# A recurrent column scan: n's bias in the tanh, z's matmuls ahead of n's, and the reset product of one half between the mix and the state of the other

## The chip, the cores and the metric

The kernel runs on one core of a Trainium2 chip. The metric is the time of one execution on the device in microseconds (us). Five engines work on their own instruction queues, each in order: TensorE (PE; its weight loads are shown apart, as PEld), VectorE (DVE), ScalarE (ACT), GpSimd (POOL) and SyncE (SP), which here only starts transfers. An instruction that waits for a semaphore holds everything behind it on its engine. Lines such as L1344 are lines of the kernel before, unless the text says that they are of the kernel after.

## The reference

The input `x` has 16 images of 32 channels and 64 x 64 pixels, in fp32. Four layers follow one another, each of the form `x = x + layer(group_norm(x))`: a 3x3 convolution, a recurrent scan over the columns of the image, and two multiplications in the Fourier domain. The change touches the scan alone:

```python
def _cell(prev_col, cur_col, weight_ih, bias_ih, weight_hh, bias_hh):
    pad = jnp.pad(prev_col, ((0, 0), (1, 1), (0, 0)))
    x = jnp.concatenate([pad[:, :-2], pad[:, 1:-1], pad[:, 2:]], axis=-1)
    i_vals = jnp.einsum('bhk,ok->bho', x, weight_ih) + bias_ih
    h_vals = jnp.einsum('bhc,oc->bho', cur_col, weight_hh) + bias_hh
    r_i, z_i, n_i = jnp.split(i_vals, 3, axis=-1)
    r_h, z_h, n_h = jnp.split(h_vals, 3, axis=-1)
    r = jax.nn.sigmoid(r_i + r_h)
    z = jax.nn.sigmoid(z_i + z_h)
    n = jnp.tanh(n_i + r * n_h)
    return n * z + cur_col * (1.0 - z)
```

Column 0 is the first state. Columns 1 to 63 each take the state of the column before (with the neighbouring pixels above and below) and their own values.

## The kernel before

**Layout.** The 128 partitions hold four interleaved row groups of 32 channels. A column of 16 images is 128 x 256 elements; it is cut into two halves of 8 images, h = 0 and 1, 128 x 128 elements each. The halves don't depend on each other. So the scan is 63 columns x 2 halves = 126 half-steps, and each engine does the halves in turn.

**One half-step** of half h and column w, by engine:

- PE (`half_step`, L700): `from_column` (L697) multiplies the current column for r, z and n into PSUM and reports `h_sum`. It waits until r's and z's gates and the reset product of the column before have been read. Then, when the state's edges (`sedge_ready`, from ACT) and its straddled copy (`lower_ready`, from POOL) are there, `from_state` (L690) multiplies the state of the column before, in three passes of four 32-column matmuls: for r, n and z, in this order; each reports its sum. In the trace a matmul in fp32 shows as two, so a pass over three gates has 24 records.
- ACT (`scan_step`, L1031), in this order in its queue: r's gate of half 0 (L1021), z's gate of half 0 (L1025), the edges of the state of half 1 of the column before (L1016), the tanh of half 0 (L1029, into PSUM), then the same with the halves exchanged.
- DVE (`new_state`, L1341), five instructions for a half: the reset product gr x PSUM (L1344), the addition with n's bias and n's sum (L1347), the keep product (z - 1) x column (L1352), the mix n x z (L1355), and the state, mix minus keep (L1360), which also waits for POOL and ACT to have read the state before it.
- POOL (`scan_step`, L527): the straddled copy of the new state, mix minus keep once more for 64 partitions (L531), as soon as mix and keep are there; then the addition of the state into the image (L525).
- SP starts two transfers per column, which bring the edge rows of a later column (L440), when both halves' `h_sum` are reported.

**What sets the order.** Nothing but the order in which the code is written for each engine, and the semaphores. DVE runs `new_state(0, w)` and then `new_state(1, w)`, three columns in a loop body, 21 times. Behind the scan DVE, ACT and POOL copy the image for the transform, when the last additions into the image (`added`) are done.

Of the kernel before, what the change touches and what calls it, by code (L numbers as in the profile page):

```python
# [15 lines left out]
ALU = mybir.AluOpType  # L16
ACT = mybir.ActivationFunctionType

B, C, H, W = 16, 32, 64, 64
# [61 lines left out]
def program(nc, x, conv_w, conv_b, scan_wi, scan_wh, scan_b, w2, w3, w9, out_b, group_d, const_d, out):  # L81
    ctx = ExitStack()
    with ctx:
        def sem(name):
            return ctx.enter_context(nc.semaphore(name))
# [16 lines left out]
        psum = ctx.enter_context(nc.psum_tensor("psum", [P, 8, 512], F32))  # L102
# [9 lines left out]
        def sm(n):  # L112
            at[0] += n
            return small[:, at[0] - n:at[0]]
# [18 lines left out]
        bias_s = sm(6)  # L133
# [5 lines left out]
        HB = B * H4 // 2  # L139
        off = 4 * H4 * PADW  # L140

        def scan_buf():
            nonlocal off
            off += HB
            return spec[:, off - HB:off]
# [11 lines left out]
        gr, gz, pre1, pre2, keep, mix = [[scan_buf() for _ in range(2)] for _ in range(6)]  # L157
        gn = [psum[:, 4 * h + 2, HB:2 * HB] for h in range(2)]
# [10 lines left out]
        def straddled(h, q, first):  # L169
            return straddle[h][q].rearrange("p (b h) -> p b h", h=H4 + 1)[:, :, first:first + H4]  # L170
# [51 lines left out]
        r_sum, z_sum, n_sum = [[sem(f"{g}_sum{h}") for h in range(2)] for g in "rzn"]  # L222
        r_gate, z_gate, n_gate = [[sem(f"{g}_gate{h}") for h in range(2)] for g in "rzn"]
        reset_done = [sem(f"reset_done{h}") for h in range(2)]
        pre_ready = [sem(f"pre_ready{h}") for h in range(2)]
# [392 lines left out]
        def _(pe):  # L618
# [53 lines left out]
            for g in range(4):  # L672
                for row in (C, 2 * C):
                    last = mm(psum[row:row + C, 5, P * g:P * g + P], bias_z[:, C * g:C * g + C], cm["ident"],
                              start=True, stop=True)
# [10 lines left out]
            def from_state(h, g, starts=False):  # L686

                moving = (straddled(h, slice(0, P), 0), state[h], state[h], straddled(h, slice(0, P), 1))
                for hm in (1, 2, 0, 3):
                    last = mm(psum[QUARTERS[hm], 4 * h + g, 0:HB], sv[:, g, QUARTERS[hm]], moving[hm],  # L690
                              start=starts, stop=True)
                return last

            def from_column(h, g, parity, stops=False):
                up, lo = edges_of(h, parity)
                for q, e in zip(QUARTERS, (up, up, lo, lo)):
                    last = mm(psum[q, 4 * h + g, 0:HB], sv[:, 3 + g, q], e, start=True, stop=stops)  # L697
                return last

            def half_step(h, w, parity, nth):  # L700
                if nth is None:
                    pe.wait_ge(cur_first[h], 32)
                else:
                    pe.wait_ge(cur_in[parity], nth * 32)
                    pe.wait_ge(r_gate[h], w - 1)
                    pe.wait_ge(z_gate[h], w - 1)
                    pe.wait_ge(reset_done[h], w - 1)
                from_column(h, 0, parity)
                from_column(h, 1, parity)
                from_column(h, 3, parity, True).then_inc(h_sum[h], 1)  # L710
                pe.wait_ge(sedge_ready[h], w)
                pe.wait_ge(lower_ready[h], w)
                from_state(h, 0).then_inc(r_sum[h], 1)
                from_state(h, 2, True).then_inc(n_sum[h], 1)
                from_state(h, 1).then_inc(z_sum[h], 1)

            pe.wait_ge(scan_w_in, 16 * 14)
            pe.wait_ge(bias_written, 2)
            pe.wait_ge(conv_added, 2 * B)
            half_step(0, 1, 1, None)  # L720
            pe.wait_ge(stat1, (NG - 1) * KGN + steps_all(GB - 1) + steps_all(1))
            half_step(1, 1, 1, None)
            with pe.Fori(0, (W - 4) // 4) as i:
                for k in range(4):
                    for h in range(2):
                        half_step(h, i * 4 + (k + 2), k % 2, i * 2 + (k // 2 + 1))
# [209 lines left out]
        def _(act):  # L936
            a = nc.scalar.activation
# [59 lines left out]
            for row, o in ((C, slice(P // 2, P)), (2 * C, slice(0, P // 2))):  # L997
# [11 lines left out]
                    bias=sh1[:, GB - 1:GB]).then_inc(columns_ready, 1)  # L1009
# [16 lines left out]

            def candidate(h, w):
                act.wait_ge(pre_ready[h], w)
                a(gn[h], pre2[h], ACT.Tanh).then_inc(n_gate[h], 1)  # L1029

            def scan_step(w):  # L1031
                reset_gate(0, w)
                update_gate(0, w)
                state_edges(1, w - 1)
                candidate(0, w)
                reset_gate(1, w)
                update_gate(1, w)
                state_edges(0, w)
                candidate(1, w)
# [140 lines left out]
        def _(dve):  # L1180
            v = nc.vector
# [156 lines left out]
                    dve.wait_ge(columns_ready, B)  # L1338
                v.tensor_copy(state[h], columns[:, h * HB:h * HB + HB]).then_inc(state_ready[h], 1)

            def new_state(h, w):  # L1341
                dve.wait_ge(r_gate[h], w)
                dve.wait_ge(h_sum[h], w)
                v.tensor_tensor(pre1[h], gr[h], psum[:, 4 * h + 3, 0:HB], ALU.mult).then_inc(reset_done[h], 1)  # L1344
                dve.wait_ge(reset_done[h], w)
                dve.wait_ge(n_sum[h], w)
                v.scalar_tensor_tensor(out=pre2[h], in0=psum[:, 4 * h + 2, 0:HB], scalar=bias_s[:, 2:3], in1=pre1[h],  # L1347
                                       op0=ALU.add, op1=ALU.add).then_inc(pre_ready[h], 1)
                dve.wait_ge(z_gate[h], w)
                dve.wait_ge(lower_ready[h], w)  # L1350

                v.scalar_tensor_tensor(out=keep[h], in0=gz[h], scalar=1.0, in1=columns[:, ds(w * (2 * HB) + h * HB, HB)],  # L1352
                                       op0=ALU.subtract, op1=ALU.mult).then_inc(keep_ready[h], 1)
                dve.wait_ge(n_gate[h], w)
                v.tensor_tensor(mix[h], gn[h], gz[h], ALU.mult).then_inc(mix_ready[h], 1)  # L1355
                dve.wait_ge(mix_ready[h], w)
                dve.wait_ge(keep_ready[h], w)
                dve.wait_ge(added[h], w)
                dve.wait_ge(sedge_ready[h], w)
                v.tensor_tensor(state[h], mix[h], keep[h], ALU.subtract).then_inc(state_ready[h], 1)  # L1360

            with dve.Fori(0, (W - 1) // 3) as i:
                for k in range(3):
                    for h in range(2):
                        new_state(h, i * 3 + (k + 1))


            dve.wait_ge(added[0], W)
# [90 lines left out]
            for half_ in range(2):  # L1459
                dve.wait_ge(l2_done, 2 * half_ + 2)  # L1460
                dve.wait_ge(sq_done, 2 * half_ + 3)
                if half_ == 0:

                    v.scalar_tensor_tensor(out=sq[0:C, :], in0=o[:, 0, 0, :], scalar=1.0, in1=shift[0:C, :],
                                           op0=ALU.mult, op1=ALU.add).then_inc(l2_added, 1)
# [6 lines left out]
                for sign, ri, dst in ((0.5, 0, col0[:, lo:hi, 0, :]), (0.5, 1, col0[:, lo:hi, 1, :]),  # L1472
# [3 lines left out]
                                           op0=ALU.mult, op1=ALU.add).then_inc(l2_added, 1)  # L1476
# [11 lines left out]
            def settle3():  # L1488
# [20 lines left out]
                                         op0=ALU.mult, op1=ALU.add))  # L1509
# [112 lines left out]
```

## Time and profile before

| | |
|---|---|
| median of 3 runs (lowest, highest) | 597.79 us (596.89, 597.91) |
| the profiled execution, its own time | 597.76 us |
| its span, first to last instruction | 595.9 us |
| mean granted TensorE clock | 0.988 of full speed |
| PE busy over the span | 539.8 us (91%) |
| DVE busy | 492.0 us (83%) |
| ACT busy | 396.7 us (67%) |
| POOL busy | 311.3 us (52%) |

The shares are means over stages with different limits, so they don't say what one stage is bound by. Inside the scan one looks at what each engine waits for: rows of a timeline give the start (us from the span's start), the duration, the engine, the line, the operation, what is written and read, and in brackets how long the engine had been idle and who released it. Where one engine's row starts a few hundredths behind another's end again and again, the two are links of a loop.

### The profile page before, as it was taken

How to read it: one execution, taken by the hardware profiler on the slowest of the kernel's cores; microseconds unless marked ns; L12 is line 12 of the kernel's file. 1: busy time of each engine (PE TensorE's matmuls, PEld its weight loads, DVE VectorE, ACT ScalarE, POOL GpSimd, SP SyncE). 2: the span in 40 equal slices, each digit the busy share in tenths (PEclk: the TensorE clock that was granted, in tenths of full speed). 3: DMA queues.
4: the chain of work that ended last, by engine and by line, in shares of the span. 5: the costliest groups of instructions: out<-in, count | busy, mean ns of one | idle time of the engine just before them, and what ended most of it. 6: DMA issues, size and time to landing. Idle time of an engine off the chain costs nothing.

```text
span 595.9 us, 26842 instructions
## 1 busy us (share of the span) xinstructions
PE 539.8 (91%) x10404; PEld 429.0 (72%) x10404; DVE 492.0 (83%) x1273; ACT 396.7 (67%) x897; POOL 311.3 (52%) x425
## 2 busy tenths in 40 slices
PE   3999999699999999999999999988889778999996
PEld 2333333477777777777777999987577667899995
DVE  7778977479989898989898787798899999377876
ACT  3445879767777776777778966676378966756441
POOL 7665654156666666666665302035799799121000
PEclk9999999899999999999999999999999997999999
DMA  6900000011111111111113100003158775003324
GB/s 226 383 6 0 2 2 4 14 39 44 40 40 44 38 41 44 36 44 40 40 44 103 50 2 0 0 2 85 60 151 248 213 227 158 31 1 142 141 123 159
DMA packets 21284, 45.69 MB, mean 77 GB/s; under 512 B 5104, under 2 KB 15600, under 8 KB 20352
## 3 DMA queue, kind: packets, MB, share of 16 engines
q1 hardware_dynamic: 20160, 44.97, 24.2%
q8 instruction: 25, 0.41, 0.3%
q10 hardware_dynamic: 672, 0.15, 0.1%
q0 software_dynamic: 416, 0.07, 0.1%
q14 instruction: 11, 0.09, 0.0%
HBM read 28.53 MB, written 8.39 MB: 62 GB/s over the span
## 4 chain that ended last, share of the span: by engine, by line
DVE 40%; PE 36%; issue 14%; ACT 6%; DVEq 2%; DMA 1%; SPq 0%; ACTq 0%
PE psum L655 8%; DVE spec L1352 8%; DVE work L338 7%; DVE spec L1344 6%; DVE spec L1355 5%; PE psum L770 5%; PE psum L909 5%; PE psum L925 5%; PE psum L786 4%; DVE small L1237 3%; PE psum L898 3%; PE psum L754 2%; ACT work L295 2%; PE psum L828 2%; DVE spec L1347 2%
## 5 line engine op out<-in xcount | busy, mean ns | idle before, releaser
L690 PE MATMUL psum<-spec,matrices 128*32 128x128 f32 x3024 | 110.0, 279 | 14.4 <-ACT spec L1016 7.5
L690 PEld LDWEIGHTS psum<-spec,matrices 128*32 128x32 f32 x3024 | 76.5, 110 | 46.6 <-ACT spec L1016 46.5
L531 POOL TENSOR_TENSOR spec<-spec 64x128 f32<-64x128 f32 x126 | 70.6, 560 | 72.1 <-DVE spec L1355 72.1
L697 PE MATMUL psum<-spec,matrices 128*32 128x128 f32 x3024 | 107.4, 274 | 0.7 <-DMA spec<-work 0.6
L697 PEld LDWEIGHTS psum<-spec,matrices 128*32 128x32 f32 x3024 | 85.6, 111 | 3.7 <-issue 3.6
L828 PE MATMUL psum<-work 128*32 128x128 f32 x2368 | 74.8, 281 | 14.8 <-ACT work L350 10.2
L655 PE MATMUL psum<-spec,matrices 128*64 128x512 f32 x384 | 86.4, 607 | 1.1 <-ACT spec L950 1.1
L828 PEld LDWEIGHTS psum<-work 128*32 128x32 f32 x2368 | 65.7, 113 | 23.7 <-issue 22.2
L338 DVE TENSOR_TENSOR work<-spec,psum 32x512 f32<-32x512 f32 x108 | 73.5, 681 | 3.8 <-PE psum L828 0.5
L509 POOL TENSOR_SCALAR spec<-image,small 32x960 f32<-32x960 f32 (+1 forms) x48 | 55.5, 1157 | 34.6 <-PE psum L655 22.0
L525 POOL TENSOR_TENSOR image<-image,spec 128x128 f32 (+1 forms) x128 | 69.4, 542 | 0.0
L655 PEld LDWEIGHTS psum<-spec,matrices 128*64 128x64 f32 x384 | 27.1, 139 | 53.8 <-issue 50.7
L350 ACT ACTIVATE work<-work 32x256 f32<-32x256 f32 x111 | 46.0, 414 | 14.7 <-DVE work L338 12.4
L1352 DVE SCALAR_TENSOR_TENSOR spec<-spec,work 128x128 f32<-128x128 f32 x126 | 54.5, 432 | 0.5 <-ACT spec L1025 0.3
L338 POOL TENSOR_TENSOR work<-spec,small 32x512 f32<-32x512 f32 x36 | 45.9, 1276 | 14.7 <-DVE small L1445 6.7
L950 ACT ACTIVATE spec<-image,small 96x1024 f32<-96x1024 f32 (+1 forms) x32 | 39.6, 1236 | 19.0 <-PE psum L655 17.5
L1029 ACT ACTIVATE psum<-spec 128x128 f32<-128x128 f32 x126 | 35.5, 282 | 23.5 <-DVE spec L1347 17.3
L1347 DVE SCALAR_TENSOR_TENSOR spec<-psum,small,spec 128x128 f32<-128x128 f32 x126 | 44.3, 351 | 4.5
L1025 ACT ACTIVATE spec<-psum 128x128 f32<-128x128 f32 x126 | 34.9, 277 | 17.1 <-PE psum L690 17.0
L1021 ACT ACTIVATE spec<-psum 128x128 f32<-128x128 f32 x126 | 35.0, 278 | 15.5 <-PE psum L690 10.0
L1237 DVE BATCH_NORM_STATS2 small<-image 128x6 f32<-128x512 f32 x64 | 40.1, 682 | 4.4 <-DMA image<-x_dram 3.3
L405 ACT ACTIVATE work<-psum 64x512 f32<-64x512 f32 x32 | 24.4, 762 | 29.0 <-PE psum L909 28.6
(154 smaller groups left out, 935.5 us busy)
## 6 DMA issues: line engine op xcount, KB each, us to landing
work<-w_dram SPq DMA_DIRECT2D x33, 512.0 KB, 4.2
spec<-work SPq DMA_DIRECT2D x124, 64.0 KB, 1.9
image<-x_dram SPq DMA_DIRECT2D x3, 2048.0 KB, 11.7
out_dram<-image SPq DMA_DIRECT2D x3, 2048.0 KB, 6.3
image<-x_dram SPq DMA_DIRECT2D x4, 512.0 KB, 5.8
work<-w_dram SPq DMA_DIRECT2D x1, 2048.0 KB, 7.7
out_dram<-image SPq DMA_DIRECT2D x4, 512.0 KB, 2.9
kept<-const_dram SPq DMA_DIRECT2D x1, 192.0 KB, 5.5
```

The source lines that it names most:

```text
L338: return multiply(dst, src, scale, ALU.mult)
L350: return activation(d[:, :, 0, m, :], d[:, :, 2, m, :], ACT.Copy, scale=-1.0)
L509: nc.gpsimd.tensor_scalar(to, of, sc0[j % 2][q, u:u + 1], sh0[j % 2][q, u:u + 1], ALU.mult, ALU.add).then_inc(norm_pool, 1)
L525: nc.gpsimd.tensor_tensor(col, col, state[h].unsqueeze(2), ALU.add).then_inc(added[h], 1)
L531: nc.gpsimd.tensor_tensor(straddled(h, ROWS_01, 0), *of, ALU.subtract).then_inc(lower_ready[h], 1)
L655: last_mm = mm(psum[o, n % 4, :], cv[:, kx, o], rows_[:, 8 * half:8 * half + 8, kx:kx + W], start=kx == 0, stop=kx == 2)
L690: last = mm(psum[QUARTERS[hm], 4 * h + g, 0:HB], sv[:, g, QUARTERS[hm]], moving[hm], start=starts, stop=True)
L697: last = mm(psum[q, 4 * h + g, 0:HB], sv[:, 3 + g, q], e, start=True, stop=stops)
L828: last = mm(o, wt[:, t, r, :], pl[:, t, from_:to], start=starts and k == 0 and r == 0, stop=r == 1, skip_group_check=True)
L1237: v.bn_stats(bnv[:, at_:at_ + 6], image[:, ds(j * (GB * ROWS) + 512 * k, 512)]).then_inc(half_sem, 1)
L1347: v.scalar_tensor_tensor(out=pre2[h], in0=psum[:, 4 * h + 2, 0:HB], scalar=bias_s[:, 2:3], in1=pre1[h], op0=ALU.add, op1=ALU.add).then_inc ...
L1352: v.scalar_tensor_tensor(out=keep[h], in0=gz[h], scalar=1.0, in1=columns[:, ds(w * (2 * HB) + h * HB, HB)], op0=ALU.subtract, op1=ALU.mult ...
```

## The change

The scan's work stays the same but for one operand; the order changes on PE and DVE.

- n's bias moves out of DVE's addition, which becomes a plain addition of two tensors, into the tanh on ACT, as its bias of one column.
- On PE `from_state` runs for r, z, n instead of r, n, z.
- On DVE `new_state` is cut into three functions. `reset_product` (the first instruction) of a half is issued behind `mixed` (addition, keep, mix) of the other half and ahead of that half's `new_state` (the state alone). The first reset product stands ahead of the loop, the last column behind it, without a product for a next column. The loop body has two columns, 31 times.

```diff
@@ half_step, PE @@
                 from_state(h, 0).then_inc(r_sum[h], 1)
+                from_state(h, 1).then_inc(z_sum[h], 1)
                 from_state(h, 2, True).then_inc(n_sum[h], 1)
-                from_state(h, 1).then_inc(z_sum[h], 1)
@@ candidate, ACT @@
-                a(gn[h], pre2[h], ACT.Tanh).then_inc(n_gate[h], 1)
+                a(gn[h], pre2[h], ACT.Tanh, bias=bias_s[:, 2:3]).then_inc(n_gate[h], 1)
@@ DVE @@
-            def new_state(h, w):
+            def reset_product(h, w):
                 dve.wait_ge(r_gate[h], w)
                 dve.wait_ge(h_sum[h], w)
                 v.tensor_tensor(pre1[h], gr[h], psum[:, 4 * h + 3, 0:HB], ALU.mult).then_inc(reset_done[h], 1)
+
+            def mixed(h, w):
                 dve.wait_ge(reset_done[h], w)
                 dve.wait_ge(n_sum[h], w)
-                v.scalar_tensor_tensor(out=pre2[h], in0=psum[:, 4 * h + 2, 0:HB], scalar=bias_s[:, 2:3], in1=pre1[h],
-                                       op0=ALU.add, op1=ALU.add).then_inc(pre_ready[h], 1)
+                v.tensor_tensor(pre2[h], pre1[h], psum[:, 4 * h + 2, 0:HB], ALU.add).then_inc(pre_ready[h], 1)
...
                 v.tensor_tensor(mix[h], gn[h], gz[h], ALU.mult).then_inc(mix_ready[h], 1)
+
+            def new_state(h, w):
                 dve.wait_ge(mix_ready[h], w)
                 dve.wait_ge(keep_ready[h], w)
                 dve.wait_ge(added[h], w)
                 dve.wait_ge(sedge_ready[h], w)
                 v.tensor_tensor(state[h], mix[h], keep[h], ALU.subtract).then_inc(state_ready[h], 1)
 
-            with dve.Fori(0, (W - 1) // 3) as i:
-                for k in range(3):
-                    for h in range(2):
-                        new_state(h, i * 3 + (k + 1))
+
+            def step(w, last=False):
+                mixed(0, w)
+                reset_product(1, w)
+                new_state(0, w)
+                mixed(1, w)
+                if not last:
+                    reset_product(0, w + 1)
+                new_state(1, w)
+
+            reset_product(0, 1)
+            with dve.Fori(0, (W - 2) // 2) as i:
+                for k in range(2):
+                    step(i * 2 + (k + 1))
+            step(W - 1, True)
```

DVE's queue in the loop of before, one column: each half runs from its reset product (L1344) to its state (L1360). The rows give line, operation, output and inputs, and the semaphores waited for; the number at a semaphore's name is the half, and an ISA row computes the column's address.

```order
L1344 TENSOR_TENSOR spec<-spec,psum 128x128 [waits h_sum0,r_gate0]
L1347 SCALAR_TENSOR_TENSOR spec<-psum,small,spec 128x128 [waits n_sum0,reset_done0]
L1352 ISA [waits lower_ready0,z_gate0]
L1352 SCALAR_TENSOR_TENSOR spec<-spec,work 128x128
L1355 TENSOR_TENSOR spec<-psum,spec 128x128 [waits n_gate0]
L1360 TENSOR_TENSOR spec<-spec 128x128 [waits added0,sedge_ready0,keep_ready0,mix_ready0]
L1344 TENSOR_TENSOR spec<-spec,psum 128x128 [waits h_sum1,r_gate1]
L1347 SCALAR_TENSOR_TENSOR spec<-psum,small,spec 128x128 [waits n_sum1,reset_done1]
L1352 ISA [waits lower_ready1,z_gate1]
L1352 SCALAR_TENSOR_TENSOR spec<-spec,work 128x128
L1355 TENSOR_TENSOR spec<-psum,spec 128x128 [waits n_gate1]
L1360 TENSOR_TENSOR spec<-spec 128x128 [waits added1,sedge_ready1,keep_ready1,mix_ready1]
```

The state of half 0 is ahead of everything of half 1. In the kernel after, the same column on DVE, with that kernel's lines (L1349 the addition, L1353 keep, L1356 mix, L1344 the reset product, L1363 the state):

```order
L1349 TENSOR_TENSOR spec<-spec,psum 128x128 [waits n_sum0,reset_done0]
L1353 ISA [waits lower_ready0,z_gate0]
L1353 SCALAR_TENSOR_TENSOR spec<-spec,work 128x128
L1356 TENSOR_TENSOR spec<-psum,spec 128x128 [waits n_gate0]
L1344 TENSOR_TENSOR spec<-spec,psum 128x128 [waits h_sum1,r_gate1]
L1363 TENSOR_TENSOR spec<-spec 128x128 [waits added0,sedge_ready0,keep_ready0,mix_ready0]
L1349 TENSOR_TENSOR spec<-spec,psum 128x128 [waits n_sum1,reset_done1]
L1353 ISA [waits lower_ready1,z_gate1]
L1353 SCALAR_TENSOR_TENSOR spec<-spec,work 128x128
L1356 TENSOR_TENSOR spec<-psum,spec 128x128 [waits n_gate1]
L1342 REGISTER_ALU
L1344 TENSOR_TENSOR spec<-spec,psum 128x128 [waits h_sum0,r_gate0]
```

The reset product of half 1 (which waits for `r_gate1`) now stands between the mix and the state of half 0, and that of half 0 for the next column ahead of the state of half 1. The last column, behind the loop, is where this ends: the state of half 1 follows its mix without a product between them.

```order
L1344 TENSOR_TENSOR spec<-spec,psum 128x128 [waits h_sum1,r_gate1]
L1363 TENSOR_TENSOR spec<-spec 128x128 [waits added0,sedge_ready0,keep_ready0,mix_ready0]
L1349 TENSOR_TENSOR spec<-spec,psum 128x128 [waits n_sum1,reset_done1]
L1353 SCALAR_TENSOR_TENSOR spec<-spec,work 128x128 [waits lower_ready1,z_gate1]
L1356 TENSOR_TENSOR spec<-psum,spec 128x128 [waits n_gate1]
L1363 TENSOR_TENSOR spec<-spec 128x128 [waits added1,sedge_ready1,keep_ready1,mix_ready1]
```

So in that column only half 0's state has a product of the other half ahead of it.

## Rows read from the trace of the kernel before

**Rows 1.** Busy time by engine, the middle of the scan (us, instructions, clock, DMA).

```profile
120.00:320.00 200.00, 189.52 (x5946) 155.12 (x5936) 181.25 (x617) 141.35 (x495) 131.13 (x246) 1.00 0.17 40
```

**Rows 2.** The chain of waits from 120 to 320 us, shares by line.

```profile
by line: issue 23.6%; DVE spec L1352 23.0%; DVE spec L1344 17.0%; DVE spec L1355 16.2%; DVE spec L1347 5.3%; ACT psum L1029 2.9%; DVEq L1352 2.9%; DVE spec L1360 2.7%; PE psum L690 2.2%; DVEq L1362 1.2%; DVEq L1346 1.0%; DVEq L1343 0.6%; AC
```

**Rows 3.** Lines of the reset product and the state: durations, starts, idle before.

```profile
L1344 DVE TENSOR_TENSOR spec<-spec,psum x126: 277/280/289, 117.5 to 321.0; 128x128 f32<-128x128 f32 x126
...
  issue: 6.0, 20
  ACT spec L1021: 3.0, 2
...
L1360 DVE TENSOR_TENSOR spec<-spec x126: 291/292/294, 118.8 to 322.4; 128x128 f32<-128x128 f32 x126
```

**Rows 4.** Timeline, one turn of PE and ACT (start, duration, [idle before]).

```profile
203.89 0.86 PE L690 MATMUL psum<-spec,matrices 128*32 128x128 f32 x24
...
204.38 0.28 ACT L1021 ACTIVATE spec<-psum 128x128 f32<-128x128 f32 x1 [0.17 <-PE psum L690]
...
204.82 0.28 ACT L1025 ACTIVATE spec<-psum 128x128 f32<-128x128 f32 x1 [0.16 <-PE psum L690]
...
205.12 0.31 ACT L1016 ACTIVATE spec<-spec 64x128 f32<-64x128 f32 x1
...
205.48 0.59 PEld L690 LDWEIGHTS psum<-spec,matrices 128*32 128x32 f32 x24 [0.34 <-ACT spec L1016]
```

**Rows 5.** Timeline, one turn of DVE and POOL, with the tanh.

```profile
199.60 0.29 DVE L1355 TENSOR_TENSOR spec<-psum,spec 128x128 f32<-128x128 f32 x1
...
199.92 0.29 DVE L1360 TENSOR_TENSOR spec<-spec 128x128 f32<-128x128 f32 x1
199.97 0.56 POOL L531 TENSOR_TENSOR spec<-spec 64x128 f32<-64x128 f32 x1 [0.48 <-DVE spec L1355]
...
200.13 0.28 DVE L1344 TENSOR_TENSOR spec<-spec,psum 128x128 f32<-128x128 f32 x1
...
200.45 0.35 DVE L1347 SCALAR_TENSOR_TENSOR spec<-psum,small,spec 128x128 f32<-128x128 f32 x1
200.50 0.54 POOL L525 TENSOR_TENSOR image<-image,spec 128x128 f32 x1
...
200.72 0.46 DVE L1352 SCALAR_TENSOR_TENSOR spec<-spec,work 128x128 f32<-128x128 f32 x1
200.84 0.28 ACT L1029 ACTIVATE psum<-spec 128x128 f32<-128x128 f32 x1 [0.18 <-DVE spec L1347]
...
201.15 0.29 DVE L1355 TENSOR_TENSOR spec<-psum,spec 128x128 f32<-128x128 f32 x1
...
201.47 0.29 DVE L1360 TENSOR_TENSOR spec<-spec 128x128 f32<-128x128 f32 x1
...
201.68 0.28 DVE L1344 TENSOR_TENSOR spec<-spec,psum 128x128 f32<-128x128 f32 x1
```

**Rows 6.** Timeline behind DVE's loop branch.

```profile
197.01 0.54 POOL L525 TENSOR_TENSOR image<-image,spec 128x128 f32 x1
...
197.03 0.29 DVE L1344 TENSOR_TENSOR spec<-spec,psum 128x128 f32<-128x128 f32 x1 [0.30 <-issue]
...
197.62 0.28 DVE L1352 SCALAR_TENSOR_TENSOR spec<-spec,work 128x128 f32<-128x128 f32 x1
```

**Rows 7.** Timeline at the scan's start, half 1 of column 1.

```profile
120.08 0.28 ACT L1021 ACTIVATE spec<-psum 128x128 f32<-128x128 f32 x1 [1.60 <-PE psum L690]
120.39 0.29 DVE L1344 TENSOR_TENSOR spec<-spec,psum 128x128 f32<-128x128 f32 x1 [1.26 <-ACT spec L1021]
```

**Rows 8.** POOL's products of another stage, by form (us busy, mean ns | idle before).

```profile
L338 POOL TENSOR_TENSOR work<-spec,small 32x512 f32<-32x512 f32 x36 | 45.9, 1276 | 14.7 <-DVE small L1445 6.7 <-PE psum L828 4.6 <-DVE small L1514 2.6
L345 POOL TENSOR_TENSOR work<-spec,small 32x256 f32<-32x256 f32 x36 | 24.3, 674 | 0.0
```

## The prediction

> **What bounds the kernel now.** I read the stretches by engine first. The scan, from about 118 to 322 us, is the third of the span that the change touches; in the 200 us in its middle DVE is busy 181, PE 190, and the granted clock is 1.00, that is 2.4 GHz, its upper level [rows 1]. The chain of waits over that stretch lies almost wholly on DVE's five lines, with 23.6% of "issue" between them; no wait on ACT or PE has a large share [rows 2]. So the eye falls on DVE, and the next view must say whether DVE waits for its inputs. By the view of the reset product's line it hardly does: of 126 products only two waited for the reset gate, 3.0 us together, and 20 lost 0.30 us each at the loop's branch (6.0 us). The states themselves start from 118.8 to 322.4 us, which is the length that the change can alter [rows 3].
>
> A half-step is the work on one half of the images for one column. In the timeline two loops run at nearly the same pace.
> PE and ACT: the pass of the state starts at 203.89, z's gate at 204.82 (0.93 later, because z's matmuls are last), it ends at 205.10, only then can ACT copy the edges of the other half (205.12 to 205.43), and PE starts the next pass at 205.48. That is 1.59 us per half-step [rows 4].
> DVE and POOL: the mix ends at 199.89, POOL's straddled state starts 0.08 later and ends at 200.53, its addition into the image follows and ends at 201.04; the keep product, which began at 200.72, ends 0.14 behind that, at 201.18, takes 0.46, and the next mix starts at 201.15. From mix to mix that is 1.55 [rows 5]. That POOL holds the keep product is seen where it isn't there: behind the 0.30 of the branch, with POOL's addition done at 197.55, the same keep, begun at 197.62, takes 0.28 [rows 6].
>
> **The change part by part.**
> Bias of n in the tanh: 126 additions lose their scalar. The row of before is 0.35 (200.45); the nearest row for its new form (one operand in PSUM, one in SBUF) is the reset product, 0.28 (200.13) [rows 5]. At most 126 x 0.07 = 8.8 us of DVE time. The tanh gets a bias of one column; no row shows it, the bounds are 0 and, from its own 0.28, not more than some hundredths, and I take 0. Neither stands on the path that I find below, so I count both at 0; the cover is DVE's wait for the reset gate.
>
> z's pass ahead of n's: three passes fill the 0.93 less 0.49 between r's and z's gate, so one is 0.22; z's sum comes at 0.71 instead of 0.93, and its gate can start when r's is done, at 0.49 + 0.28 + 0.03 = 0.80 [rows 4]. The first loop falls from 1.59 to 1.46. n's sum comes 0.22 later, at 0.93, but the addition that reads it stands behind the reset product (not before 0.49 + 0.28 + 0.03 + 0.32 = 1.12), so that costs 0. This alone would not reach below the second loop, 1.55.
>
> DVE's new order: mix of one half, reset product of the other, state of the first. Nothing is added to the queue, but one in-order wait changes its place: the state of one half is now queued behind a product that waits for the other half's reset gate, and that gate is made from the other half's state, which is the state just ahead. So state n cannot start before state n-1 has gone through edges, PE, gate and product. Before, the state came first and only its own half's chain, two half-steps long, had to close. The new chain, from the start of one state to the start of the next, with the row each time:
> state 0.29 (201.47) [rows 5]; hand-off from DVE to ACT 0.04 (addition ends 200.80, tanh 200.84) [rows 5]; edges 0.31, hand-off to PE 0.05, PE's start to r's gate 0.49, gate 0.28 [rows 4]; gate to product 0.03 (120.36 to 120.39) [rows 7]; from the product to the state queued behind it 0.21, taken from 201.47 to 201.68, where a state and a product that waits for nothing follow each other [rows 5].
> Sum: 0.29 + 0.04 + 0.31 + 0.05 + 0.49 + 0.28 + 0.03 + 0.21 = 1.70 us per half-step.
>
> What could hide in it or lengthen it: ACT has z's gate of the other half ahead of the edges. It ends 0.80 + 0.28 - 0.49 = 0.59 behind the start of r's gate; the edges are wanted 0.28 + 0.03 + 0.21 + 0.29 + 0.04 = 0.85 behind it, so it is out of the way. PE needs about 1.27 of weight loads per half-step (1.59 less an idle of about 0.33), and is free. The 0.30 of the branch, now every second column instead of every third, falls into DVE's wait for the gate and costs 0 as long as that wait is there. The state's four waits may cost its queue more than 0.21: the row with all four is 0.32 from mix to state, but there 0.29 is the mix itself; I keep 0.21 and take 0.27 as the upper end, 1.76 for the sum. The lower end is 1.65, five of the eight pieces shorter by a hundredth, to which the rows are read.
>
> POOL's port in the new order: counted from the end of a state, POOL's addition runs 0.08 to 0.62, keep ends at 0.76, mix runs 0.73 to 1.02, POOL's straddled state starts at 1.10 and the next state is due to end at 1.70. If a state behind POOL ends 0.14 after it, like the keep product, it matters whether the straddled state takes 0.56, as its row says [rows 5], or less. Its row always begins 0.05 behind a state's start, so it may hold a wait. POOL's products of 512 and 256 elements take 1276 and 674 ns [rows 8], which gives 2.35 ns an element and 0.37 us for 128 (estimate). With 0.37 POOL ends at 1.47 and the state at 1.61 at the earliest: nothing lost. With 0.56 it is 1.66 and 1.80.
> The Trainium skill, "SBUF — State Buffer", Who interferes with whom, says that a DVE instruction with two SBUF inputs and a GpSimd instruction that reads SBUF exclude each other, whichever starts first. The 0.46 against 0.28 of the keep product agrees; by that rule the row of 0.56 holds a wait for the state that began 0.05 earlier, and the sum stays 1.70; if POOL's row is all its own, it is 1.80.
>
> **The sum.** The first product of the other half starts at 120.39 [rows 7], and the first state is now behind it: 120.60 instead of 118.8. 124 half-steps of 1.70 bring state 125 to 331.40. The last state has no product ahead: it comes 0.29 + 0.08 + 0.54 + 0.14 - 0.03 + 0.32 = 1.34 later, 332.74 against 322.4 [rows 3]. All later stages wait for that end, so the run gets 10.3 us longer: 597.76 of the profiled execution, which is within 0.03 of the median, becomes 608.1; I say 608.0. Even is where 120.60 + 124 p + 1.34 = 322.4, at p = 1.617.
>
> **The rivals.**
> Port (1.80): POOL's straddled state needs its whole 0.56 and holds every state. 120.60 + 223.2 + 1.34 = 345.1, 22.7 longer, 620.5. For it: the row's constant length. Against: the slope of POOL's other products, and the keep that is held in the same way.
> Hand-offs (1.60), on the other side: the rows' ends lie behind the moments at which the semaphores are posted, so a sum of rows overstates a chain of eight pieces by 0.10. It decides below 1.617. 320.3, or 2.1 less: 595.7, no slower than before. For it: PE's ends are modelled. Against: I used starts for PE, and mix to state shows 0.32 for 0.29 plus a hand-off.
> No closing of the chain (1.43): the product finds its gate ready, as it did in 124 of 126 cases before. Then half a chain of its own half decides: state to product 1.49, product to addition 0.32, addition to mix 0.63 (0.28, 0.04, tanh 0.28, 0.03), mix to product and product to state 0.21 each, 2.86 per two half-steps. 299.3, or 23.1 less: 574.7. For it: the two waits in the view. Against: the products were late enough before only because a state, an addition, a keep and a mix of the other half stood ahead; the data they need are the same.
>
> **Chances.** Forecast with 1.65 to 1.76 (602 to 616 us): 0.60. Port: 0.24. Hand-offs: 0.10. No closing: 0.06. The range, 602 to 620.5, holds the forecast's own and reaches to the port rival's time. A measurement of this kernel can tell 0.2%, 1.2 us, from no change: faster 0.12 (the fast case, and some half of the hand-offs), same 0.03, slower 0.85.
>
> **What would show it.** Right: the reset product waits for ACT's reset gate in nearly all of its 126 cases, about 0.18 us each (product at 1.49 behind the state's start, engine free at 1.31), 20 us or more in all; states 1.70 apart and alike at the branch; the addition near 0.28; z's gate 0.31 behind r's; PE's wait for the edges grown from 0.34 to about 0.43. The port rival would show states longer than 0.29, or a start-to-end of 0.4; the straddled state's row at 0.37 to 0.43 speaks against it. Wrong: products that don't wait, or states less than 1.62 apart.

## The result and the profile after

| | before | after |
|---|---|---|
| median | 597.58 us | 618.38 us |
| lowest, highest of the runs | 596.89, 597.91 | 616.64, 619.29 |
| ratio (95% interval) | | 1.0346 (1.0324 to 1.0369) |

The kernel after is slower by 20.8 us. The forecast was 608.0, the range 602 to 620.5, and the time that the port rival gave was 620.5. The profiled execution took 619.29 us. All times of runs below are medians of undisturbed executions: one of 1438.79 us, of the run with the bias on DVE and the loop written out, is left out.

First the page of the kernel after: busy time by engine, the chain of work that ended last, and the group of the reset product (count, then busy us, mean ns, idle before it and what ended most of it). Below it stands the chain from the page of the kernel before.

```profile
PE 540.0 (87%) x10404; PEld 427.9 (69%) x10404; DVE 475.4 (77%) x1273; ACT 399.2 (65%) x897; POOL 310.4 (50%) x425
...
PE 40%; DVE 28%; ACT 16%; issue 12%; DVEq 2%; DMA 0%; SPq 0%; ACTq 0%
...
L1344 DVE TENSOR_TENSOR spec<-spec,psum 128x128 f32<-128x128 f32 x126 | 36.3, 288 | 16.4 <-ACT spec L1021 3.6
```

```profile
DVE 40%; PE 36%; issue 14%; ACT 6%; DVEq 2%; DMA 1%; SPq 0%; ACTq 0%
```

DVE is busy for 16.6 us less than before (475.4 against 492.0) in a run that is 21 us longer. Over the whole span, DVE's share of the chain falls from 40% to 28% and ACT's rises from 6% to 16%: a sign that the loop, which in the scan of before lay almost all on DVE [rows 2], now closes through other engines.

The lines of the state (L1363 now) and of the addition (L1349), with minimum, median and maximum duration in ns and first and last start:

```profile
L1363 DVE TENSOR_TENSOR spec<-spec x126: 284/344/471, 120.8 to 344.6; 128x128 f32<-128x128 f32 x126
...
L1349 DVE TENSOR_TENSOR spec<-spec,psum x126: 272/275/290, 118.0 to 343.4; 128x128 f32<-128x128 f32 x126
```

States start from 120.8 to 344.6 instead of 118.8 to 322.4 [rows 3]. The last one is 22.2 us later, and the two profiled executions differ by 21.5: the whole loss lies in the scan. From state to state it is 1.79 on average (223.8 / 125), where the prediction had 1.70. And a state, always 0.29 before, now takes 0.28 to 0.47: something holds it.

One plain half-step of the kernel after, in order of time (start, duration, engine, line; idle time in brackets). This answers to [rows 4, 5]:

```profile
339.64 0.34 DVE L1363 TENSOR_TENSOR spec<-spec 128x128 f32<-128x128 f32 x1
339.91 0.27 DVE L1349 TENSOR_TENSOR spec<-spec,psum 128x128 f32<-128x128 f32 x1
340.02 0.31 ACT L1016 ACTIVATE spec<-spec 64x128 f32<-64x128 f32 x1 [0.39 <-DVE spec L1363]
340.10 0.28 DVE L1353 SCALAR_TENSOR_TENSOR spec<-spec,work 128x128 f32<-128x128 f32 x1
340.17 0.63 POOL L525 TENSOR_TENSOR image<-image,spec 128x128 f32 x1 [0.34 <-DVE spec L1363]
340.35 0.37 ACT L1029 ACTIVATE psum<-spec,small 128x128 f32<-128x128 f32 x1
340.37 0.59 PEld L690 LDWEIGHTS psum<-spec,matrices 128*32 128x32 f32 x24 [0.49 <-ACT spec L1016]
340.38 0.86 PE L690 MATMUL psum<-spec,matrices 128*32 128x128 f32 x24 [0.22 <-ACT spec L1016]
...
340.75 0.29 DVE L1356 TENSOR_TENSOR spec<-psum,spec 128x128 f32<-128x128 f32 x1 [0.37 <-ACT psum L1029]
340.87 0.28 ACT L1021 ACTIVATE spec<-psum 128x128 f32<-128x128 f32 x1
...
341.12 0.45 POOL L531 TENSOR_TENSOR spec<-spec 64x128 f32<-64x128 f32 x1 [0.32 <-DVE spec L1356]
341.18 0.29 DVE L1344 TENSOR_TENSOR spec<-spec,psum 128x128 f32<-128x128 f32 x1
341.38 0.34 DVE L1363 TENSOR_TENSOR spec<-spec 128x128 f32<-128x128 f32 x1
```

Two loops end at the second state, and both can be read from these rows.
The chain of the prediction (the gate is r's): state ends 339.98, edges 340.02 to 340.33, PE 340.37, gate 340.87 to 341.15, product 341.18, state 341.38. With a state of 0.29 it would be 0.29 + 0.04 + 0.31 + 0.04 + 0.50 + 0.28 + 0.03 + 0.20 = 1.69. The link that makes it a chain is in every half-step: all 126 products start 0.03 behind the end of their gate, where in the kernel before they started 0.03 to 0.48 behind it.
The port (by which the prediction means that POOL and DVE keep each other out while both read SBUF): edges end 340.33, only then can ACT do the tanh (340.35 to 340.72, 0.37 with the bias, where it was 0.28 [rows 5]), mix 340.75 to 341.04, POOL's straddled copy 341.12 to 341.57, and the state, begun at 341.38, ends at 341.72, 0.15 behind POOL. That is the 0.34 instead of 0.29, and 1.74 from state to state. In 123 of the 126 half-steps the state ends 0.15 behind POOL's copy.

At the branch of DVE's loop, every fourth half-step, it is worse. The same kernel at such a place:

```profile
190.85 0.34 DVE L1363 TENSOR_TENSOR spec<-spec 128x128 f32<-128x128 f32 x1
...
191.38 0.56 POOL L525 TENSOR_TENSOR image<-image,spec 128x128 f32 x1 [0.34 <-DVE spec L1363]
191.43 0.29 DVE L1349 TENSOR_TENSOR spec<-spec,psum 128x128 f32<-128x128 f32 x1 [0.24 <-issue]
191.58 0.59 PEld L690 LDWEIGHTS psum<-spec,matrices 128*32 128x32 f32 x24 [0.49 <-ACT spec L1016]
...
191.64 0.44 DVE L1353 SCALAR_TENSOR_TENSOR spec<-spec,work 128x128 f32<-128x128 f32 x1
191.75 0.37 ACT L1029 ACTIVATE psum<-spec,small 128x128 f32<-128x128 f32 x1 [0.22 <-DVE spec L1349]
192.15 0.28 ACT L1021 ACTIVATE spec<-psum 128x128 f32<-128x128 f32 x1
192.16 0.29 DVE L1356 TENSOR_TENSOR spec<-psum,spec 128x128 f32<-128x128 f32 x1
...
192.46 0.29 DVE L1344 TENSOR_TENSOR spec<-spec,psum 128x128 f32<-128x128 f32 x1
192.53 0.45 POOL L531 TENSOR_TENSOR spec<-spec 64x128 f32<-64x128 f32 x1 [0.59 <-DVE spec L1356]
192.66 0.47 DVE L1363 TENSOR_TENSOR spec<-spec 128x128 f32<-128x128 f32 x1
```

The addition comes 0.24 late, and with it the tanh (191.75 to 192.12). That has two effects. On ACT r's gate is queued behind the tanh: it starts at 192.15, 0.57 behind the weight loads instead of 0.50, and so the state starts 0.07 late. On DVE the mix starts 0.04 behind the tanh's end, 1.31 behind the state instead of 1.11; POOL's copy ends at 192.98, and the state with it at 193.13, after 0.47, which makes the next state late. (The keep product, held to 0.44 by POOL's addition into the image, which is ahead of it here, ends at 192.08, before the tanh does.) The four half-steps of a loop take 1.75, 1.74, 1.81 and 1.87.

### The profile page after: what moved, and what is told of

The parts are those of the page before. It is cut to its first block, busy times and chain, and to the rows that moved or that the text cites. A ratio compares the mean times of both kernels' runs of the same rounds, so it can differ in the third digit from the quotient of the medians.

```text
span 617.5 us, 26890 instructions
## 1 busy us (share of the span) xinstructions
PE 540.0 (87%) x10404; PEld 427.9 (69%) x10404; DVE 475.4 (77%) x1273; ACT 399.2 (65%) x897; POOL 310.4 (50%) x425
## 4 chain that ended last, share of the span: by engine, by line
PE 40%; DVE 28%; ACT 16%; issue 12%; DVEq 2%; DMA 0%; SPq 0%; ACTq 0%
DVE work L338 8%; PE psum L655 8%; PE psum L690 7%; DVE spec L1363 6%; ACT spec L1021 6%; PE psum L770 5%; PE psum L909 5%; PE psum L925 5%; ACT spec L1016 5%; DVE small L1237 3%; PE psum L786 3%; PE psum L898 2%; PE psum L754 2%; ACT work L295 2%; ACT psum L1029 2%
## 5 line engine op out<-in xcount | busy, mean ns | idle before, releaser
L525 POOL TENSOR_TENSOR image<-image,spec 128x128 f32 (+1 forms) x128 | 77.8, 608 | 43.8 <-DVE spec L1363 43.8
L531 POOL TENSOR_TENSOR spec<-spec 64x128 f32<-64x128 f32 x126 | 57.0, 453 | 51.2 <-DVE spec L1356 51.2
L1016 ACT ACTIVATE spec<-spec 64x128 f32<-64x128 f32 x127 | 38.9, 306 | 54.5 <-DVE spec L1363 54.3
L1356 DVE TENSOR_TENSOR spec<-psum,spec 128x128 f32<-128x128 f32 x126 | 36.7, 292 | 36.7 <-ACT psum L1029 34.3
L1029 ACT ACTIVATE psum<-spec,small 128x128 f32<-128x128 f32 x126 | 46.9, 372 | 9.3 <-DVE spec L1349 6.8
L1344 DVE TENSOR_TENSOR spec<-spec,psum 128x128 f32<-128x128 f32 x126 | 36.3, 288 | 16.4 <-ACT spec L1021 3.6
L1363 DVE TENSOR_TENSOR spec<-spec 128x128 f32<-128x128 f32 x126 | 46.7, 371 | 0.0
L1021 ACT ACTIVATE spec<-psum 128x128 f32<-128x128 f32 x126 | 35.0, 278 | 16.5 <-PE psum L690 2.0
```

The source lines that it names most:

```text
L525: nc.gpsimd.tensor_tensor(col, col, state[h].unsqueeze(2), ALU.add).then_inc(added[h], 1)
L531: nc.gpsimd.tensor_tensor(straddled(h, ROWS_01, 0), *of, ALU.subtract).then_inc(lower_ready[h], 1)
L1016: a(straddled(h, ROWS_23, 1), state[h][ROWS_23].rearrange("p (b h) -> p b h", h=H4), ACT.Copy).then_inc(sedge_ready[h], 1)
L1021: a(gr[h], psum[:, 4 * h, 0:HB], ACT.Sigmoid).then_inc(r_gate[h], 1)
L1029: a(gn[h], pre2[h], ACT.Tanh, bias=bias_s[:, 2:3]).then_inc(n_gate[h], 1)
```

## The experiments

Theory A says: the order alone makes a serial chain of 1.69; POOL's hold on the state, through the longer tanh and the branch, lengthens it. Its rivals: B, the loss is the bias in the tanh; C, POOL's hold alone sets the pace; D, it is the new order together with z's place.

**The state back behind its mix.** z's pass first and the bias in the tanh stay.

```diff
                 mixed(0, w)
-                reset_product(1, w)
                 new_state(0, w)
+                reset_product(1, w)
                 mixed(1, w)
-                if not last:
-                    reset_product(0, w + 1)
                 new_state(1, w)
+                if not last:
+                    reset_product(0, w + 1)
```

Expected:

> The kernel after, but with the state directly behind its mix and the other half's reset product behind the state, as before; z's pass first, n's bias in the tanh and the loop of two columns stay. Theory A (a serial chain through the product that stands ahead of the state, lengthened by POOL's hold on the state): both go with the order, half-steps fall from 1.79 on average to 1.55 plus a branch of 0.30 in four, 1.625: 597.6 + 126 x 0.012 = 599 us (596 to 602), the state's row back to 0.29, products that hardly wait. Rival B (the bias makes each tanh 0.09 longer, and that is the loss): 126 x 0.09 = 11 us stay, 609 us.

Measured: 599.39 us, ratio to before 1.0046 (1.003 to 1.0062). Its line of the state, and one tanh with the mix behind it:

```profile
L1363 DVE TENSOR_TENSOR spec<-spec x126: 291/292/294, 118.8 to 324.9; 128x128 f32<-128x128 f32 x126
...
201.54 0.37 ACT L1029 ACTIVATE psum<-spec,small 128x128 f32<-128x128 f32 x1 [0.21 <-DVE spec L1349]
...
201.95 0.29 DVE L1356 TENSOR_TENSOR spec<-psum,spec 128x128 f32<-128x128 f32 x1
```

No state is held any more, and 19.0 of the 20.8 us are gone with two instructions exchanged. B falls as the whole cause. Starts of states are 1.57 to 1.58 apart inside the loop body, not 1.55: the tanh ends last ahead of the mix, which starts a hand-off of 0.03 to 0.04 behind it in 125 of 126 half-steps, and the tanh is 0.09 longer, while the addition ahead of it is only 0.06 shorter (0.29 against 0.35).

**The bias back on DVE.** The new order and z's pass first stay.

```diff
-                v.tensor_tensor(pre2[h], pre1[h], psum[:, 4 * h + 2, 0:HB], ALU.add).then_inc(pre_ready[h], 1)
+                v.scalar_tensor_tensor(out=pre2[h], in0=psum[:, 4 * h + 2, 0:HB], scalar=bias_s[:, 2:3], in1=pre1[h],
+                                       op0=ALU.add, op1=ALU.add).then_inc(pre_ready[h], 1)
...
-                a(gn[h], pre2[h], ACT.Tanh, bias=bias_s[:, 2:3]).then_inc(n_gate[h], 1)
+                a(gn[h], pre2[h], ACT.Tanh).then_inc(n_gate[h], 1)
```

Expected:

> The kernel after, but n's bias again in DVE's addition; order and z's pass stay. Theory A: the tanh is 0.09 shorter, so mix and POOL's straddled copy come 0.09 sooner, the state is held no more (row 0.29 instead of 0.34), and the half-step falls to the bare chain, 1.69 to 1.70, some 0.02 more for the branch: 120.8 + 124 x 1.71 + 1.3 = 334.2, 609 us (606 to 613). Rival B (the bias is the whole loss): 598 us. Rival C (POOL's hold alone sets the pace and no chain stands behind it): it falls by the whole 0.09 per half-step, to 1.65 and below, under 606 us.

Measured: 613.00 us, ratio 1.0282 (1.0263 to 1.0301): 5.4 less than the kernel after. A plain half-step:

```profile
201.40 0.28 DVE L1364 TENSOR_TENSOR spec<-spec 128x128 f32<-128x128 f32 x1
...
201.72 0.31 ACT L1016 ACTIVATE spec<-spec 64x128 f32<-64x128 f32 x1 [0.34 <-DVE spec L1364]
...
202.05 0.28 ACT L1029 ACTIVATE psum<-spec 128x128 f32<-128x128 f32 x1
202.08 0.59 PEld L690 LDWEIGHTS psum<-spec,matrices 128*32 128x32 f32 x24 [0.44 <-ACT spec L1016]
...
202.57 0.28 ACT L1021 ACTIVATE spec<-psum 128x128 f32<-128x128 f32 x1 [0.24 <-PE psum L690]
...
202.74 0.45 POOL L531 TENSOR_TENSOR spec<-spec 64x128 f32<-64x128 f32 x1 [0.17 <-DVE spec L1357]
...
202.88 0.29 DVE L1344 TENSOR_TENSOR spec<-spec,psum 128x128 f32<-128x128 f32 x1 [0.23 <-ACT spec L1021]
203.09 0.29 DVE L1364 TENSOR_TENSOR spec<-spec 128x128 f32<-128x128 f32 x1
```

The product waits 0.23 for the reset gate, the state isn't held, and the spacing is the bare chain, 1.69. It did not fall below, as C would have it. The total is 4 us above what A expected, because the branch, which I put at 0.02, still costs: the half-steps around it are 1.78 and 1.87, with a state of 0.47 between them.

**POOL copies the finished state.** The order, z's place and the bias of the kernel after stay; POOL's loop is written out.

```diff
-                pool.wait_ge(mix_ready[h], w)
-                pool.wait_ge(keep_ready[h], w)
-                of = [t[h][ROWS_01].rearrange("p (b h) -> p b h", h=H4) for t in (mix, keep)]
-                nc.gpsimd.tensor_tensor(straddled(h, ROWS_01, 0), *of, ALU.subtract).then_inc(lower_ready[h], 1)
                 pool.wait_ge(state_ready[h], w + 1)
+                pool.wait_ge(straddle_zeroed, 1)
+                nc.gpsimd.tensor_copy(straddled(h, ROWS_01, 0), state[h][ROWS_01].rearrange("p (b h) -> p b h", h=H4)
+                                      ).then_inc(lower_ready[h], 1)
```

Expected:

> The kernel after, but POOL makes the straddled copy from the finished state (one input, 64 partitions) instead of mix minus keep, and POOL's loop is written out; so POOL reads nothing while DVE's state runs. Theory A: the state's row is 0.29 throughout, and the chain through the reset product alone is left, the 1.70 of the prediction with the branch hidden: 608 to 610 us. Rival C (POOL's hold alone): without it nothing keeps the half-steps from edges 0.35, tanh 0.39, mix to state 0.41 and the state's 0.29, 1.47: 581 us.

Measured: 617.48 us, ratio 1.0355 (1.0338 to 1.0372). A missed the number by 8 us, C by 36. (C's pieces, as they stand, add up to 1.44 and not 1.47, so its miss is larger still.) The rows of one half-step (lines of this kernel: L1359 the state, L1012 the edges, L530 the copy, L1349 keep, L1352 the mix, L1017 r's gate, L1340 the product):

```profile
200.73 0.28 DVE L1359 TENSOR_TENSOR spec<-spec 128x128 f32<-128x128 f32 x1
...
201.05 0.31 ACT L1012 ACTIVATE spec<-spec 64x128 f32<-64x128 f32 x1 [0.34 <-DVE spec L1359]
201.08 0.28 POOL L530 COPY spec<-spec 64x128 f32<-64x128 f32 x1 [0.98 <-DVE spec L1359]
201.13 0.89 DVE L1349 SCALAR_TENSOR_TENSOR spec<-spec,work 128x128 f32<-128x128 f32 x1
201.33 0.54 POOL L525 TENSOR_TENSOR image<-image,spec 128x128 f32<-128x128 f32 x1
...
201.51 0.86 PE L686 MATMUL psum<-spec,matrices 128*32 128x128 f32 x24 [0.26 <-POOL spec L530]
201.94 0.28 DVE L1352 TENSOR_TENSOR spec<-psum,spec 128x128 f32<-128x128 f32 x1
201.99 0.28 ACT L1017 ACTIVATE spec<-psum 128x128 f32<-128x128 f32 x1 [0.24 <-PE psum L686]
...
202.30 0.29 DVE L1340 TENSOR_TENSOR spec<-spec,psum 128x128 f32<-128x128 f32 x1
202.50 0.28 DVE L1359 TENSOR_TENSOR spec<-spec 128x128 f32<-128x128 f32 x1
```

No state is held (all 126 are 0.28 to 0.29), and yet the half-step is 1.77 to 1.78. PE now waits for POOL: copy and edges both end at 201.36, and the state's matmuls start at 201.51, 0.15 later; in the kernel after, where POOL's copy is long done, they start 0.05 behind the edges (340.33, 340.38). State 0.28, hand-off 0.07, copy 0.28, hand-off 0.15, PE to gate 0.48, gate 0.28, 0.03, product to state 0.20: 1.77. It is the same chain with POOL's leg in the place of ACT's. POOL's hold is not gone altogether: it now falls on the keep product (0.89), and so the mix is late. But the product starts 0.36 behind the mix, and 0.03 behind the gate, as in all 126 half-steps: it is the gate that it waits for. So with no state held the chain sets the pace, which C can't give; what I had missed in the expectation is POOL's slower hand-off to PE.

**DVE's loop written out**, nothing else changed against the kernel after.

```diff
-            with dve.Fori(0, (W - 2) // 2) as i:
-                for k in range(2):
-                    step(i * 2 + (k + 1))
+            for w in range(1, W - 1):
+                step(w)
```

Expected:

> The kernel after with DVE's loop over the columns written out, nothing else changed. Theory A with the branch not hidden: all half-steps are 1.74 as inside the loop body now, 120.8 + 124 x 1.743 + 1.3 = 338.2 against 344.6 now: 612 us. If the branch is hidden in the wait for the gate, as the prediction had it: no change, 618 us.

Measured: 613.71 us, ratio 1.0291 (1.0273 to 1.031), 4.7 less than the kernel after. 113 of 125 spacings are 1.74 or 1.75: the branch was not hidden.

**The new order alone**, on the kernel before (with the new order's loop of two columns): n's matmuls ahead of z's again and the bias on DVE, so the run with the bias on DVE and this one differ in z's place only. The edit against that run:

```diff
                 from_state(h, 0).then_inc(r_sum[h], 1)
-                from_state(h, 1).then_inc(z_sum[h], 1)
                 from_state(h, 2, True).then_inc(n_sum[h], 1)
+                from_state(h, 1).then_inc(z_sum[h], 1)
```

Expected:

> The kernel before with DVE's new order alone (and its loop of two columns): n's matmuls ahead of z's, n's bias in DVE's addition. Theory A (the order alone makes the loss): z's gate, now 0.22 later, still ends 0.1 ahead of the edges that are queued behind it, so the chain is the same 1.69 as with z's pass first, with the branch 1.75 on average: 613 us (609 to 617). Rival D (the new order needs, or suffers from, z's pass ahead of n's): more than 3 us away from the 613.0 of the run with the bias back on DVE. Rival B (bias) would have 597.6.

Measured: 614.66 us, ratio 1.0289 (1.0272 to 1.0306). Inside the loop body states are 1.68 to 1.69 apart, as with z first. D falls: the order does it alone, 17.1 us behind the kernel before (597.54 in this set of runs).

**Bias on DVE and loop written out**, the two edits above together, on the kernel after; what is left is the new order and z's place.

Expected:

> The kernel after with n's bias again in DVE's addition and DVE's loop written out: both things that lengthened the bare chain are gone, the new order and z's pass stay. Theory A: all half-steps 1.69, states 0.29, products waiting about 0.23 each; 120.5 + 124 x 1.69 + 1.4 = 331.5, some 9 us behind before: 606 us (604 to 609), the sum of the prediction less what its pieces were rounded up by. If something else than the chain held the half-step it would not stay at 1.69: under 600 us or over 612.

Measured: 607.99 us, ratio 1.0169 (1.0147 to 1.0191), 10.4 above before. Its lines of the state and of the product (the last row: us and times that the product waited for r's gate):

```profile
L1364 DVE TENSOR_TENSOR spec<-spec x126: 284/285/442, 121.3 to 333.5; 128x128 f32<-128x128 f32 x126
...
L1344 DVE TENSOR_TENSOR spec<-spec,psum x126: 286/289/290, 118.2 to 332.0; 128x128 f32<-128x128 f32 x126
...
  ACT spec L1021: 30.6, 122
```

117 of 125 spacings are 1.68 or 1.69, and the product waits for the gate 122 times. Here one sees the bare chain of the prediction, and nearly its time. (It is 2 us above the expectation: the first state came at 121.3 rather than 120.5, and two half-steps of 2.02 and a few of 1.8 remain.)

**z's pass first alone**, on the kernel before.

Expected:

> The kernel before with z's pass ahead of n's alone. Reading of the trace of before: two loops side by side, PE and ACT 1.59 and DVE and POOL 1.55 with a branch in six half-steps. With z first the former falls to 1.46 and only the latter is left, so the 0.39 that a branch costs in before falls to 0.30: 21 x 0.09 = 2 us less, 595.7 (594 to 597.6). If z's loop were no bound at all: no change.

Measured: 597.03 us, ratio 0.999 (0.998 to 1.0001): no difference that can be told. The spacings stayed 1.55 with 1.94 or 1.95 at the branch.

**Two versions without the new order.** DVE's loop of the kernel before written out (`for w in range(1, W): for h in range(2): new_state(h, w)`), once with z's pass first and once without it.

Expected with z first:

> The kernel before with z's pass ahead of n's and DVE's loop written out; DVE's order and the bias as before. If POOL's port and the tanh set 1.55 and PE's loop is at 1.46: 21 branches of 0.39 go, 8 us: 589.5 us (587 to 593), faster than both kernels. If PE's and ACT's 1.59 stayed: 594.5.

Measured: 590.45 us, ratio 0.9888 (0.9873 to 0.9903), states mostly 1.55 apart.

Expected without:

> The kernel before with DVE's loop written out and nothing else: n's matmuls still ahead of z's. If the trace of before is read rightly as two loops, PE and ACT with z last at 1.59 are now what is left, and writing the loop out brings only 126 x (1.615 - 1.59) = 3 us: 594.5 us (593 to 596.5). If POOL's port and the tanh alone set the pace, it falls to 1.55 like the run with z's pass first: 590.5.

Measured: 594.64 us, ratio 0.9951 (0.9936 to 0.9966), states mostly 1.59 apart. The rows that set it, PE's pass, the two gates and the edges behind z's gate:

```profile
199.35 0.86 PE L690 MATMUL psum<-spec,matrices 128*32 128x128 f32 x24
...
199.84 0.28 ACT L1021 ACTIVATE spec<-psum 128x128 f32<-128x128 f32 x1 [0.24 <-PE psum L690]
...
200.28 0.28 ACT L1025 ACTIVATE spec<-psum 128x128 f32<-128x128 f32 x1 [0.16 <-PE psum L690]
...
200.58 0.31 ACT L1016 ACTIVATE spec<-spec 64x128 f32<-64x128 f32 x1
...
200.94 0.59 PEld L690 LDWEIGHTS psum<-spec,matrices 128*32 128x32 f32 x24 [0.34 <-ACT spec L1016]
```

199.35 to 200.94 is the 1.59 of [rows 4]. So PE's and ACT's loop was read rightly, and z's place is worth 4 us, but only once the branch is gone. The version with both is the fastest of all, 7.1 us under the kernel before. It is also the partner of the run with the bias on DVE and the loop written out, which differs from it in DVE's order alone: 590.45 against 607.99, 1.55 against 1.69 per half-step. That is the price of the new order by itself, 17.5 us.

## Why the prediction was right, and where it was off

**The direction and the step that makes it** were right: the state queued behind a product that waits for the gate made from the state just ahead. The forecast's sum was 1.70, the bare chain is 1.68 to 1.69 in three experiments, and with bias and branch out of the way the kernel is 10.4 us behind before where the sum gave 10.3. (Both numbers are taken against a kernel that has its own branches in the loop; without them the order costs the 17.5.)

**The time in the range is in part luck.** The forecast's own band, 602 to 616, does not hold 618.38. The range does, because it was drawn out to the port rival's time; the reason given for that time, a copy of 0.56, did not hold, and two terms taken at 0 happened to cost nearly as much.

**Two terms were mis-sized**, and they make the other half of the loss.
- The tanh's bias, "not more than some hundredths, and I take 0", is 0.09 (0.37 against 0.28), and costs 5.4 us here (618.38 against 613.00) and 5.7 with the loop written out (613.71 against 607.99). The cover that I named, DVE's wait for the gate, does hide the tanh from DVE's product; but behind the mix stands POOL's copy, and what makes POOL late holds the state. The prediction did not see it because it had POOL's addition hold the keep product until 0.76 behind the state's end, and the mix behind that. In the kernel after keep starts before POOL's addition (340.10, 340.17) and is done at 0.40; the mix, at 0.77, starts 0.03 behind the tanh. The Trainium skill, "ScalarE: Activation LUTs", What ACT_TABLE_LOAD costs, states that a bias given as a column adds about 93 ns to an activation; the trace's 0.09 agrees. I had not weighed it.
- The branch, "falls into DVE's wait for the gate and costs 0", costs 4.7 us (618.38 against 613.71), or 5.0 with the bias on DVE (613.00 against 607.99). By the prediction's own numbers, a wait of 0.18 and a branch of 0.30, the cover was too small. It comes in by two ways: the late tanh keeps r's gate waiting on ACT (1.81 instead of 1.74), and the late mix makes POOL late, which holds the state (0.47 instead of 0.34, and the 1.87).

Taken off one after the other, the bias 5.4, the branch 5.0 and what is left, 10.4, make the 20.8. That sum closes by itself, since each part is the difference of two medians; with the branch taken off first it is 4.7, 5.7 and 10.4. The kernel before had 596.72 us in one set of runs and 597.54 in the other, so each part is good to about 1 us.

**The second loop of the kernel before** was rightly put at 1.55, but not by the links that the prediction named, POOL's addition and the keep product that it holds. The mix starts 0.03 behind the end of the tanh (201.12, 201.15), in 125 of 126 half-steps, and 0.03 before keep has ended (201.18) [rows 5]. The links are mix to state 0.32, to product 0.21, to addition 0.32, to tanh 0.39, to mix 0.31, together 1.55; POOL's hold on keep runs beside them with a few hundredths to spare. So the tanh stood on one of the two paths that set the pace already before the change.

**The port rival** was half right: its time was the nearer one, and states are held, but not because POOL's copy needs 0.56. It needs 0.45, between my 0.37 and the row's 0.56; that row did hold a wait for the state in front of it. With 0.45 and the mix as early as I had it, nothing would have been held, as the run with the bias on DVE shows in its plain half-steps. The rule that was weighed, of the Trainium skill, "SBUF — State Buffer", Who interferes with whom, is that DVE with two SBUF inputs and POOL reading SBUF exclude each other, whichever starts first. The traces agree both ways round: a copy that starts before the state takes 0.45 and the state ends 0.15 behind it, and a copy that starts 0.05 behind the state takes 0.56.

**The other rivals** fell: no spacing came under 1.68 with the new order, but for the last, which has no product ahead of its state; neither shorter hand-offs nor products that find their gate ready were seen.

**The signs that I had named.** The addition is 0.275 as said. The product's idle time is 16.4 us over the scan, not 20: in a plain half-step it is 0.14 (341.04 to 341.18), since the longer tanh brings the mix later; with the bias on DVE it is 0.23. PE waits 0.49 for the edges (0.43 said). z's gate starts 0.22 behind r's (340.87, 341.09), not 0.31: it started 0.06 before r's had ended, where I had it wait for that end. "States alike at the branch" was wrong.

**z's pass first** was rightly priced at no gain by itself here: 597.03 against 597.54.

## What to carry to other kernels

An instruction moved ahead of another in an in-order queue takes its waits with it: write down the loop from what the moved instruction waits for to what is now queued behind it, and if that loop closes over one round where it closed over two before, the pipelining of the two halves is gone. Free time of an engine covers a longer instruction only if nothing else, such as a port held by a third engine, is fed by that instruction. Several loops of nearly equal length hide each other: z's place was worth nothing until the branch was taken out of the loop beside it.

## What the runs showed of the hardware that was not expected

- A tanh of 128 x 128 with a column as its bias took 372 ns, without it 282.
- DVE's keep product took 0.28 alone, 0.44 to 0.48 in the kernel before, where one POOL instruction had started before it (it ends 0.14 to 0.15 behind that one), and 0.89 where POOL's copy and its addition ran back to back: it did not get in between the two, and ended 0.15 behind the second. The other way round, POOL's addition into the image took 0.63 instead of 0.54 to 0.56 where keep had started before it, and 0.70 in the run with the bias on DVE.
- From the end of POOL's copy to PE's first matmul it was 0.15, from the end of ACT's edges 0.05.
- The loop's branch cost DVE 0.24 to 0.30 each time. Written out, the code had a few pauses instead: two half-steps of 2.02 to 2.07 in 125 in the written-out versions with the new order. Their cause stays open.
